# Splitting the skip and gate steps of a state-space scan across two state rows, and issuing the B-row broadcasts later

## The reference, cut to what matters

```
dA  = exp(dt[..., None] * A)                 # 512 channels x 16 state rows n
dBx = dt[..., None] * Bc[:, :, None, :] * xc[..., None]
h   = dA_t * h + dBx_t                       # along time, for each channel and n
y   = sum over n of h[n] * C[n]
y   = y + Dp * xc                            # "skip"
y   = y * silu(z)                            # "gate"
```

## Time and profile before

| what | value |
|---|---|
| device time, median of 3 runs | 6363.51 us (6357.47 to 6367.97) |
| profiled execution: device time | 6367.97 us |
| profiled execution: span | 6366.2 us |
| `scans`, first to last instruction | about 3821 to 5207 us of the span |
| one pair in the steady part (skip to skip on VectorE) | 84.87 us |
| VectorE busy over the span | 4670.8 us (73%) |
| GpSimd (POOL) busy over the span | 3699.2 us (58%) |

### The profile page before, as it was taken

One profiled execution on the slowest core, in us unless ns is written; L12 is line 12 of the kernel. 1 busy time (PEld: TensorE's weight loads), 2 busy tenths in 40 slices (PEclk: granted clock), 3 DMA queues, 4 the chain that ended last, 5 costly groups with the idle time before them and its releaser, 6 DMA issues. The chain is left out here.

```text
span 6366.2 us, 126141 instructions
## 1 busy us (share of the span) xinstructions
PE 5502.0 (86%) x40354; PEld 3579.2 (56%) x40354; DVE 4670.8 (73%) x6108; ACT 4439.8 (70%) x7115; POOL 3699.2 (58%) x2063
## 2 busy tenths in 40 slices
PE   3688888888888888888879977999999979999999
PEld 3466666666666666665534434555555546666665
DVE  1688988888888888888878958999999961221221
ACT  1698998989899898999936668888888851111111
POOL 2677777777777777777610008999999960000000
PEclk7899999999999999999989989999999999999999
DMA  1212111121211212120035556555555541111110
GB/s 34 43 27 46 29 37 35 27 47 26 47 27 28 45 26 48 28 45 18 13 120 189 213 187 217 204 186 206 189 199 202 206 164 34 33 33 49 33 33 10
DMA packets 470082, 538.37 MB, mean 85 GB/s; under 512 B 251056, under 2 KB 345008, under 8 KB 469568
## 3 DMA queue, kind: packets, MB, share of 16 engines
q1 hardware_dynamic: 469568, 531.63, 27.3%
HBM read 370.18 MB, written 161.35 MB: 83 GB/s over the span
## 5 line engine op out<-in xcount | busy, mean ns | idle before, releaser
L317 DVE CUSTOM_DVE_ANT_0 srow<-srow,ps_s,cur 128x1024 f32<-128x1024 f32 x1024 | 1304.0, 1273 | 262.9 <-PE ps_s L465 180.8
L394 ACT ACTIVATE srow<-srow,nmax 128x1024 f32<-128x1024 f32 x1024 | 1190.9, 1163 | 207.6 <-DVE nmax L317 195.0
L403 ACT COPY AT<-ps_t 128x512 f32<-128x512 f32 x2048 | 1104.9, 597 | 74.8 <-PE ps_t L476 74.0
L476 PEld LDWEIGHTS ps_t<-ident,srow 128*128 128x128 f32 x8192 | 962.7, 143 | 279.1 <-ACT AT L403 84.1
L476 PE MATMUL ps_t<-ident,srow 128*128 128x128 f32 x8192 | 1105.0, 279 | 13.1 <-ACT AT L403 8.7
L1725 POOL TENSOR_TENSOR c_hc<-c_hs,c_cs 128x1024 f32<-128x1024 f32 x432 | 1009.8, 2363 | 60.8 <-DVE c_hs L1827 58.9
L465 PE MATMUL ps_s<-K,Q 96*128 96x512 bf16 x2048 | 632.3, 391 | 440.3 <-DVE nmax L317 318.5
L306 DVE SCALAR_TENSOR_TENSOR srow<-ps_p,rho,R 128x1024 f32<-128x1024 f32 x768 | 975.4, 1270 | 13.7 <-ACT ps_p L357 9.2
L1686 PE MATMUL c_ps_y<-c_hc,c_ident 128*128 128x512 f32 x2048 | 944.8, 594 | 30.0 <-POOL c_hc L1725 17.1
L1827 DVE TENSOR_TENSOR_SCAN c_hs<-c_da,c_pd 128x1024 f32<-128x1024 f32 x384 | 860.2, 2274 | 54.6 <-PE c_pd L1677 54.0
L1770 ACT ACTIVATE c_sT<-c_dxT,c_bT 128x256 f32<-128x256 f32 x1536 | 668.4, 494 | 106.8 <-PE c_pd L1677 96.6
(11 more groups left out here) (196 smaller groups left out, 8361.8 us busy)
## 6 DMA issues: line engine op xcount, KB each, us to landing
c_cs<-bc_d SPq DMA_DIRECT2D x256, 512.0 KB, 4.3
c_bs<-bc_d SPq DMA_DIRECT2D x64, 512.0 KB, 6.7
parts_d<-parts SPq DMA_DIRECT2D x65, 384.0 KB, 3.3
K<-parts_d SPq DMA_DIRECT2D x192, 128.0 KB, 4.6
Q<-parts_d SPq DMA_DIRECT2D x384, 64.0 KB, 2.9
sz_d<-b_sz SPq DMA_DIRECT2D x16, 1024.0 KB, 7.1
xv_d<-b_xv SPq DMA_DIRECT2D x16, 1024.0 KB, 7.7
dt_d<-b_ab SPq DMA_DIRECT2D x16, 1024.0 KB, 4.2
```

What stands on the lines that cost most here:

```text
L317: nc.vector.tensor_tensor_reduce(r[:], r[:], ps_s[:], cur[k][:, h:h + 1], BIG, ALU.add, ALU.min, nmax[:, h % NROW:h % NROW + 1]).then_inc( ...
L394: nc.scalar.activation(r[:], r[:], ACT.Exp, scale=-1.0, bias=nmax[:, h % NROW:h % NROW + 1]).then_inc(e_ok, 1)
L403: nc.scalar.copy(AT[h % NAT][:, HG * half:HG * half + HG, :], ps_t[:, half]).then_inc(at_ok, 1)
L476: last = nc.tensor.transpose(ps_t[:, half, i, :], rows_sb[h % NROW][:, j * P:(j + 1) * P], ident[:])
```

## The change

Three edits, all in `scans`.

1. VectorE's skip step writes into `y` in SBUF where it wrote back into `ps_y` in PSUM. TensorE may start the next pair's sums after the skip (`y_step`) and no longer after the gate (`y_ok`).
2. The gate is done one row later, at n = 3, as y = y · sz, both in SBUF; before it read `ps_y` in PSUM and `sz`.
3. SP fetches a row of B two rows ahead and after `spread_c` and `load`, where it was four rows ahead and in front of `spread_c`. So row 5 is asked for at n = 3 behind the four loads (before: at n = 1), row 9 at n = 7, row 13 at n = 11, and row 1 of the next pair at n = 15.

```
             def store(q, b, p):
...
-                alone(sp, y_ok, 2 * q + 2 + 2, sp_own)
+                alone(sp, y_ok, 2 * q + 2, sp_own)
...
                 for n in range(NS):
-                    if n + 4 in ROWS_N and n > 0:
-                        spread_b(q, b, n + 4)
-                    if n + 4 == NS + ROWS_N[0] and not last:
-                        spread_b(q + 1, next_b, ROWS_N[0])
                     spread_c(q, b, n)
...
                             store(q - 1, b - 1 + p, 1 - p)
                             load_end(q, b, p)
+                    if n + 2 in ROWS_N and n > 0:
+                        spread_b(q, b, n + 2)
+                    if n == NS - 1 and not last:
+                        spread_b(q + 1, next_b, ROWS_N[0])
...
             def sums(q, n, c):
                 if n == 0:
-                    pe.wait_ge(y_ok, 2 * q + c + 1)
+                    pe.wait_ge(y_step, 2 * q + c + 1)
...
-            dve.sem_inc(y_ok, 2)
+            dve.sem_inc(y_step, 2)
...
                 if c == 0:
                     dve.wait_ge(e_in, 32 * q + 32)
-                nc.vector.scalar_tensor_tensor(ps_y[:, c, :], xv[:, c, :], d_p[:, 2 * p + c, :], ps_y[:, c, :],
+                    dve.wait_ge(stored, 16 * q + 16)
+                nc.vector.scalar_tensor_tensor(y[:, c, :], xv[:, c, :], d_p[:, 2 * p + c, :], ps_y[:, c, :],
                                                ALU.mult, ALU.add).then_inc(y_step, 1)
 
             def gated(q, c):
-                if c == 0:
-                    dve.wait_ge(stored, 16 * q + 16)
-                dve.wait_ge(y_step, 2 * q + c + 1)
-                nc.vector.tensor_tensor(y[:, c, :], ps_y[:, c, :], sz[:, c, :], ALU.mult).then_inc(y_ok, 1)
+                dve.wait_ge(y_step, 2 * q + c + 1 + 2)
+                nc.vector.tensor_tensor(y[:, c, :], y[:, c, :], sz[:, c, :], ALU.mult).then_inc(y_ok, 1)
...
                         if not first and n == 2:
                             with_skip(q - 1, 1 - p, c)
+                        if not first and n == 3:
                             gated(q - 1, c)
...
             for c in range(2):
                 with_skip(PAIRS * B - 1, PAIRS - 1, c)
+            for c in range(2):
                 gated(PAIRS * B - 1, c)
```

## The result

The changed kernel takes 6411.53 us (median of four runs, 6406.79 to 6412.49) where the kernel before takes 6360.49 (four runs, 6357.11 to 6367.97): 51 us more, a ratio of 1.0078 with a 95% interval of 1.0059 to 1.0095. The direction was the one forecast. The size was twice the one forecast (24 us), and the time lies at the upper end of the range of 6362 to 6411.

A forecast was written before the change was run, and what follows sets the result against it. VectorE was taken to set each pair. Nine pairs at 15.75 us and five at 8.2 made 24 us, added to the median of 6363.5 and rounded to 6388 us; range 6362 to 6411.

The forecast's parts named there:

- VectorE sets the pair, GpSimd follows: In `scans`, VectorE sets the 84.87 us of a pair; GpSimd follows with 3.6 us of slack.
- Edit 1 gains 0.2 us a pair and nothing more: Skip followed by scan instead of the dependent gate: 0.1 us saved twice a pair; TensorE's earlier start worth nothing.
- Row 5 is late and reaches VectorE through the ring: Late `bs` delays GpSimd; scan (5,1) reuses the ring buffer of (3,1) and waits, in fourteen pairs.
- L: Lateness of row 5's `bs` against GpSimd's start of L1718: 1.6 to 5.2 us over pairs 1 to 14.
- the sum: Lateness estimate per pair: issue of the transfer behind the loads, plus landing, minus the start of L1718.
- L - 2.75: VectorE's cost at scan (5,1) after 2.75 us of ring slack; 15.75 us over nine pairs, L counted at least 4.2.
- nothing gives it back: After late scan (5,1), the 0.3 us transpose waits in rows 7 and 8 move along, so no lateness is recovered.
- A gate waits for one instruction of GpSimd: A moved gate with two SBUF inputs waits only for the rest of GpSimd's running instruction, 0 to 2.33 us.
- a rival with a chance of 0.1: GpSimd passes a waiting gate as long as it has work ready: 66 us, 6430; chance 0.1.
- five pairs with L below 3.0: Pairs where gate 1 finds `times_b` of (5,0) begun and waits for its end, L - 0.7 each: 8.2 us.
- holds it: Gate 1 finds GpSimd idle and holds it until 4114.6, so L counts as at least 4.2; nine pairs.
- a row in time: Rival: row 5's `bs` lands by GpSimd's need, gates cost 0.25 and 0.2 a pair: 6361 to 6367 us; chance 0.17.

The follow-up runs named there:

- Experiment 8: Kernel before, with VectorE's skip replaced by TensorE matmuls of a diagonal matrix of D with xv, added to its sums at rows 8 and 12: 6331.98 us, ratio 0.995.
- experiment 4: experiment 1 with the gate replaced by a sum over y alone, one SBUF input, at the same place, output not gated: 6371.91 us, ratio 1.0014.
- experiment 5: experiment 4 with four matmul passes of a zero matrix added to TensorE's sums of (2,1): 6362.32 us, ratio 0.9999.
- experiment 2: Kernel before with only the later fetch of B rows, two rows ahead and behind the loads: 6389.39 us, ratio 1.0045.
- experiment 7: Kernel before with row 9 of B issued at n = 4, right behind the four loads: 6360.79 us in one run.
- experiment 1: Changed kernel with the later fetch undone, rows of B four ahead again; skip into SBUF and later gate kept: 6463.17 us, ratio 1.0159.
- experiment 3: Changed kernel with row 5 of B issued right before the four loads, other rows left two ahead: 6466.97 us, ratio 1.016.
- experiment 6: Changed kernel with B rows early and both gates after unit (9,1), store and loads of xv and sz at n = 11: 6379.2 us, ratio 1.003.

## Why the prediction was half right

**VectorE sets the pair, GpSimd follows: right.** Experiment 8 takes 2.5 us from VectorE alone and a pair gets 2.0 shorter; the waits keep their shape.

**Edit 1 gains 0.2 us a pair and nothing more: right.** It is 0.27 in the even pairs of experiment 4, and skip to scan takes 1.17 in the changed kernel (4111.54, 4112.71), forecast as 1.19. What the prediction did not see is a cost of it. TensorE's sums no longer wait for the gates, so TensorE is done 1.8 us sooner, and it is idle for 2.8 us ahead of row 6 where it was for 1.24. Where the granted clock falls behind that, a scan waits about 1 us. In the changed kernel one pair (q = 2) shows such a wait, 0.95 us. In experiment 4 odd pairs do, and filling the idle time (experiment 5) took 9.6 us off. The late row can do the same without edit 1: in experiment 2 a scan of q = 6 waits 0.62 for transposes behind idle time of TensorE of 2.7 us.

**Row 5 is late and reaches VectorE through the ring: right in its mechanism, wrong in its size.** In the prediction's sense (start of L1718, minus skip 0, minus 7.21) L is 4.95, 5.2, 4.52, 6.17, 3.51, 6.7, 3.97, 3.73, 6.46, 7.16, 3.47, 6.13, 4.5 and 8.92 us for q = 1 to 14: 5.4 in the mean, where the prediction had 3.6. The pair with 8.92 shows it best:

```profile
5084.22 2.35 POOL L1718 TENSOR_TENSOR c_db<-c_dx,c_bs 128x1024 f32<-128x1024 f32 x1 [9.19 <-DMA c_bs<-bc_d]
```

The issue was where it was put, 7.2 us behind that of the first load in the mean. Two things were longer. The row landed 8.4 us after its issue in the mean (7.2 to 10.5) instead of the 6.8 of the `cs` row that stood in that place, and `times_b` started 0.3 after the landing (4122.96 to 4123.27 at q = 3), which the sum had at nothing. Where L is large, part of the wait falls on scan (5,0), which needs the late product itself (at q = 14 it waits 2.87 us and scan (5,1) another 3.30), and the sum of both is again L - 2.75 (6.17).

L - 2.75 over the fourteen pairs is 36.9 us, and 34.2 were measured, but this agreement is in part chance. Ten pairs grow by 0.35 to 0.45 us less than L - 2.75 (q = 3 by 1.34 for 1.77), and so do eleven pairs of experiment 2, without edit 1. So "nothing gives it back" was wrong by 0.4 us a pair: at q = 3, of VectorE's three waits for transposes of 0.3 us behind scan (5,1), one is gone and one is down to 0.09. And the 0.2 of edit 1 is not saved on top, since it lies ahead of the wait. The other four pairs grow by more than that rule: q = 2 by 3.7 for 2.45, through the wait for transposes just named, and q = 5, 8 and 11 because gate 1 does meet `times_b` there (below). The 14 pairs were forecast to cost 24.

Why the row lands later there is open: a `bs` row in nearly the same place, but for another row of B, took 7.6 (experiment 7), the `cs` row of experiment 1 took 7.2, and the late row of experiment 2 took 8.0. The landing may hang on what the other transfers do at that moment; no run here shows it.

**A gate waits for one instruction of GpSimd: wrong.** This is the step that failed in its mechanism; the lateness above was only mis-sized. The prediction took the price of a collision as 0 to 2.33 us from the one collision that the trace had, where GpSimd had nothing ready. It said that no row showed the other case, took the cheap one, and left the dear one to a rival with a chance of 0.1. With GpSimd's next instruction ready, the gate loses every time: 15 gates of 8.2 to 8.3 us in experiment 1, 15 in experiment 3, one in the changed kernel. With nothing ready it gets in after the instruction that runs (gate 0 of the changed kernel, 1.32 to 1.42 in twelve pairs; experiment 6, 3.60 for two). Pair 15, forecast at nothing, cost 6.7 us by this. The Trainium skill (SBUF — State Buffer, "Who interferes with whom") says that a VectorE instruction with two SBUF inputs contends with a GpSimd instruction that reads SBUF, and of VectorE's two-port modes that whoever issues first gets the shared pair for the whole instruction. The first half agrees with experiment 4, where one input was enough to bring the gate back to 1.19 us. The second, carried over to this gate, does not: the gate asked 0.27 us before GpSimd's next instruction began (4115.99, 4116.26) and still came behind it and two more. Why GpSimd keeps the access between two instructions no run here shows.

**Why the collision cost so little in the changed kernel.** The prediction let gate 1 collide in five pairs with L below 3.0. No L was below 3.47, so that branch was never taken, and its 8.2 us are not in the result. Where L was least, `times_b` began 0.4 to 0.7 us after gate 1 and took 2.93, 2.66 and 2.99 us (q = 5, 8 and 11): the prediction's "holds it", for 0.3 to 0.6 us. Gate 0, which would have met three ready instructions, found GpSimd standing for the row. The late row hides the collision: 100 us alone, 26 for the late row alone, 51 together. Experiment 3 shows it the other way round. That the time came out at the end of the range and not far beyond it is luck: for a row in time the prediction had 6361 to 6367 us, and experiment 1 took 6463.

**The signs it named.** `times_b` waits for the transfer in 14 pairs: right, but 78 us, not 45 to 60. VectorE waits for GpSimd, up to 3.3 us: right. The gate's mean over 1.22 with a spread to 3: the mean is 1.49, but by one gate of 8.23; the other 31 lie between 1.19 and 1.42. Pairs of 86.5: 87.3. No wait came at rows 9 or 13.

The 40.7 us in `scans` and the 3.1 ahead of it are, within 0.4, the 43.4 between the two profiled executions; to the 51 between the medians the rest is the 7.5 by which the profiled execution of the kernel before lay over its median.

## What to carry to other kernels

Before an operation is moved from PSUM to SBUF, count the SBUF inputs that it then has, and look what GpSimd has ready at that moment: a VectorE instruction with two SBUF inputs is not delayed by one GpSimd instruction but by all that it can run without VectorE, three here. A stall can hide another cost, so of two faults in one change the removal of one can make it slower; run each edit alone before one is blamed. And where a row stands behind a batch of loads on one queue, take the worst landing seen in that place, not the mean, since the lateness comes out one for one beyond the slack; here even the worst before, 7.9 us, lay below the 8.4 that came in the mean. Taking a step off the engine that sets the time (here the skip, as a matmul with a diagonal on TensorE, 30 us) was worth more than any rearrangement of it that was tried.

## What the runs showed of the hardware

- GpSimd, with instructions ready back to back, keeps a waiting VectorE instruction with two SBUF inputs out for all of them: 8.2 to 8.3 us for one of 1.2, through three more instructions of 2.35, in 31 of 31 gates that came so. With nothing ready behind, the wait ends with the instruction that runs: 1.37 us for a gate that asked 0.29 before its end, 3.60 for two that asked 1.4 before.
- The other way the loss is about what is left of the gate: a GpSimd product that began 0.26 us into a gate of 1.19 took 3.14 to 3.15 us instead of 2.35, 0.8 longer, with 0.94 of the gate left.
- With one SBUF input, at the same place, the VectorE instruction shows nothing (1190 to 1212 ns over 32), nor does the gate with one input in PSUM and one in SBUF (1224 to 1225).
- After idle time of TensorE of 2.8 us the granted clock was 1.00 over ten us in one pair and 0.83 in the next, eight transposes taking 1.09 and 1.97 us. With more work for TensorE, so that it was idle for 1.07 us there, the clock was 1.00 in every pair and the kernel 9.6 us faster.
- A 512 KB row issued behind 3.1 MB of loads landed after 7.2 to 10.5 us in the changed kernel; the issue of the last load itself held SyncE for 4.2 to 6.2.
